# Four slots for gathered expert rows and a new timetable for scatters and expert tiles in a cross-attention and MoE kernel

## What is computed

```python
def reference(x, ctx_4096, L0_ffn_base_w, L0_ffn_base_b, L0_ffn_A, L0_ffn_B, L0_ffn_router_w):
    # x (8, 224, 2048), ctx (8, 750, 2048), base_w (2048, 2048), A (64, 2048), B (16, 2048, 64), all fp32
    def _L0_xattn_ref(query, key):
        a = jnp.einsum('bqd,bkd->bqk', query, key)
        e = jax.nn.softmax(a, axis=-1)
        return jnp.einsum('bqk,bkd->bqd', e, key)
    def _L0_ffn_ref(x, base_w, base_b, A, B, router_w):
        base_out = jnp.einsum('bsi,oi->bso', x, base_w) + base_b
        res_hidden = jnp.einsum('bsi,ri->bsr', x, A)
        probs = jax.nn.softmax(jnp.einsum('bsi,ei->bse', x, router_w), axis=-1)
        topw, topi = jax.lax.top_k(probs, 2)
        topw = topw / (jnp.sum(topw, axis=-1, keepdims=True) + 1e-06)
        combine = jnp.sum(jax.nn.one_hot(topi, 16, dtype=x.dtype) * topw[..., None], axis=-2)
        delta = jnp.einsum('bse,bsr,eor->bso', combine, res_hidden, B)
        return base_out + delta * 0.5
    x = x + _L0_xattn_ref(_layernorm(x, axis=-1), ctx_4096)
    x = x + _L0_ffn_ref(_layernorm(x, axis=-1), L0_ffn_base_w, L0_ffn_base_b, L0_ffn_A, L0_ffn_B, L0_ffn_router_w)
    return x
```

## Time and profile before

| | us |
|---|---|
| median of three runs | 1538.42 (1529.47 to 1540.98) |
| the profiled execution | 1535.22 |
| its span, first to last instruction | 1533.5 |
| PE busy | 1386.5 |
| VectorE busy | 948.0 |
| ACT busy | 630.4 |
| POOL busy | 319.4 |
| mean granted clock of TensorE | 0.957 |

### The profile page before, as it was taken

How to read it: one execution, slowest core, us unless ns; L and a number is a source line. 1 busy time by engine, 2 the same in 40 slices (tenths; PEclk the granted TensorE clock), 3 DMA queues, 4 the chain that set the end, 5 groups by cost and what they waited for, 6 DMA issues and landing times.

```text
span 1533.5 us, 18405 instructions
## 1 busy us (share of the span) xinstructions
PE 1386.5 (90%) x6777; PEld 1121.6 (73%) x6777; DVE 948.0 (62%) x1199; ACT 630.4 (41%) x797; POOL 319.4 (21%) x247
## 2 busy tenths in 40 slices
PE   5889999999999999998997779877788999999998
PEld 4668787777878787876886657755566778888886
DVE  5467777677776867774572646554557664555543
ACT  3354554545455555453210546554556621011100
POOL 1001102020202020103217323334344111111110
PEclk9989999999999999998999889888898999999999
DMA  6967778686878686695645698797886788888884
GB/s 226 272 195 248 218 245 259 206 257 209 251 236 263 218 266 215 209 218 171 196 137 159 191 300 228 201 297 209 246 260 169 250 290 262 240 240 244 259 256 130
DMA packets 216840, 350.59 MB, mean 229 GB/s; under 512 B 26992, under 2 KB 129392, under 8 KB 207088
## 3 DMA queue, kind: packets, MB, share of 16 engines
q1 hardware_dynamic: 198192, 282.31, 61.0%
q0 software_dynamic: 10528, 52.85, 11.4%
q10 hardware_dynamic: 8064, 14.68, 2.8%
HBM read 266.11 MB, written 99.41 MB: 238 GB/s over the span
## 4 chain that ended last, share of the span: by engine, by line
PE 32%; DMA 12%; DVE 4%; ACT 3%; issue 2%; POOL 2%; SPq 1%; ACTq 0%; POOLq 0%; DVEq 0%
PE scores L821 10%; PE scores L822 9%; PE scores L823 9%; DMA b_in<-in_bT_dram,brow_i 6%; DMA res<-x_scratch 4%; ACT b_hl L1029 2%; POOL hs_scratch L1566 1%; PE work L857 1%; DMA w_in<-in_wT_dram 1%; PE work L858 1%; DVE b_hl L1410 1%; DVE a_l L1368 1%; SPq L561 1%; DVE w_l L1361 1%; DMA a_in<-xT_scratch 1%
## 5 line engine op out<-in xcount | busy, mean ns | idle before, releaser
L821 PE MATMUL scores<-w_h,a_h 128*128 128x512 f32 x896 | 359.0, 401 | 60.8 <-DVE a_l L1368 56.6
L822 PE MATMUL scores<-w_l,a_h 128*128 128x512 f32 x896 | 355.1, 396 | 0.0
L823 PE MATMUL scores<-w_h,a_l 128*128 128x512 f32 x896 | 354.8, 396 | 0.0
L821 PEld LDWEIGHTS scores<-w_h,a_h 128*128 128x128 f32 x896 | 171.8, 192 | 103.8 <-DVE a_l L1368 51.3
L1014 ACT ACTIVATE a_h<-a_in 128x512 fp32r<-128x512 f32 x168 | 93.9, 620 | 314.6 <-DMA a_in<-xT_scratch 204.6
L1368 DVE TENSOR_TENSOR a_l<-a_in,a_h 128x512 fp32r<-128x512 f32 x168 | 130.4, 824 | 124.8 <-ACT a_h L1014 120.6
L823 PEld LDWEIGHTS scores<-w_h,a_l 128*128 128x128 f32 x896 | 171.2, 191 | 38.9
L822 PEld LDWEIGHTS scores<-w_l,a_h 128*128 128x128 f32 x896 | 171.8, 192 | 37.6
L691 PE MATMUL scores<-ctxT_h,nT_h 128*112 128x494 f32 (+1 forms) x512 | 175.0, 342 | 10.1 <-DVE ctxT_l L1119 6.7
L1129 DVE TENSOR_TENSOR raw_l<-raw_in,val_h 128x512 fp32r<-128x512 f32 x192 | 154.9, 826 | 45.5 <-ACT val_h L945 45.3
L790 PE MATMUL scores<-val_h,eT_h 128*112 128x512 f32 (+1 forms) x384 | 159.5, 415 | 19.2 <-DVE raw_l L1129 17.5
(11 more groups left out here) (153 smaller groups left out, 1903.6 us busy)
## 6 DMA issues: line engine op xcount, KB each, us to landing
ctxT_in<-in_ctxT_dram SPq DMA_DIRECT2D x64, 750.0 KB, 6.6
a_in<-xT_scratch SPq DMA_DIRECT2D x42, 1024.0 KB, 9.4
raw_in<-in_ctx_dram SPq DMA_DIRECT2D x32, 1280.0 KB
w_in<-in_wT_dram SPq DMA_DIRECT2D x32, 512.0 KB, 11.1
x<-in_x_dram SPq DMA_DIRECT2D x8, 1792.0 KB, 10.6
xT_scratch<-xT_st SPq DMA_DIRECT2D x8, 1792.0 KB, 11.8
res<-x_scratch SPq DMA_DIRECT2D x56, 256.0 KB, 7.9
y_add<-y_scratch SPq DMA_DIRECT2D x56, 256.0 KB, 5.5
```

The source lines that it names most:

```text
L821: pe.matmul(o, ah, wh, start=(k == 0), stop=False)
L822: pe.matmul(o, ah, wl, start=False, stop=False)
L823: last = pe.matmul(o, al, wh, start=False, stop=(k == KD - 1))
```

## The change

`b_in` spans all 128 partitions and has four slots: tiles with s % 4 of 0 and 1 use partitions 0 to 63, tiles with 2 and 3 partitions 64 to 127, and `b_hl` takes the high part on the same half and the low part on the other (`halves`). Four gathers are issued at once in the beginning, two in visit 11, and later each gather stands six tiles ahead. The 28 scatters of hidden rows stand in visits 6 to 9 instead of 7 to 10, each in the same groups of seven. The first group of hidden rows is loaded and transposed in visit 11 instead of 10, and `expert_high` and `expert_low` of tiles 0 and 1 stand ahead of `slots_high(0)` and `slots_low(0)`. Visit 11 joins `ROUTING`. The tiles of visits 11 to 15 were 3, 3, 0, 0, 4 and are 0, 2, 2, 3, 3; visits 16 to 26 keep three each.

```diff
@@ -89,6 +89,7 @@
     ACCS = 3
     SL = (2 * T + E * (P - 1)) // P
     SG = 4
+    BR = 4
     GROUPS = -(-SL // SG)
     RW = R + 1
     NOWHERE = 4096
@@ -261,7 +262,7 @@
         b_hl = over(at_x2, "b_hl", [P, 2, D], F32R)
         masked = over([at_nT[0]], "masked", [P, E, E])
         ends_at = over([at_nT[0] + 4 * E * E], "ends_at", [R, SL, E])
-        b_in = over(at_nT, "b_in", [R, 2, D])
+        b_in = over(at_nT, "b_in", [P, 2, D])
         routes = list(at_nT)
         y_out = over(at_nT, "y_out", [P, 3, D])
         s_hh = over(at_nT, "s_hh", [P, 2, SG * P], F32R)
@@ -314,6 +315,11 @@
 
         acc = [scores[:, 1, 0:BANK], scores[:, 1, BANK:2 * BANK], scores[:, 0, 0:BANK]]
         s_bank = scores[:, 0, BANK:2 * BANK]
+
+        def halves(s):
+
+            same, other = slice(0, R), slice(R, P)
+            return (same, other) if s % BR < 2 else (other, same)
 
         def y_bank(c):
             return work[:, c // 2, (c % 2) * BANK:(c % 2 + 1) * BANK]
@@ -385,7 +391,7 @@
         s_high = sem("s_high")
         s_ready = sem("s_ready")
         yrow_ready = sem("yrow_ready")
-        b_loaded = [sem(f"b_loaded{i}") for i in range(2)]
+        b_loaded = [sem(f"b_loaded{i}") for i in range(BR)]
         b_high = sem("b_high")
         b_ready = sem("b_ready")
         y_done = sem("y_done")
@@ -410,17 +416,17 @@
 
         X2T_TAIL_AT = (2, 5, 8, 11)
         HID_TAIL_AT, HN_TAIL_AT = 1, 6
-        HR_AT, ROUTE_AT, COUNT_AT, PLACE_AT, SCATTER_AT = 3, 4, 6, 6, (7, 8, 9, 10)
-        Y_FIRST_AT = 10
-        ROUTING = (ROUTE_AT, ROUTE_AT + 1, PLACE_AT)
+        HR_AT, ROUTE_AT, COUNT_AT, PLACE_AT, SCATTER_AT = 3, 4, 6, 6, (6, 7, 8, 9)
+        Y_FIRST_AT = 11
+        ROUTING = (ROUTE_AT, ROUTE_AT + 1, PLACE_AT, Y_FIRST_AT)
 
         Y_TILES, n = {}, 0
-        for g in (11, 12) + tuple(range(TT + 1, 2 * TT - 1)):
-            count = min(4 if g == TT + 1 else 3, SL - n)
+        for g in range(TT - 2, 2 * TT - 1):
+            count = min(2 if g < TT else 3, SL - n)
             Y_TILES[g] = list(range(n, n + count))
             n += count
         assert n == SL
-        Y_BEHIND = {3: (3, 8, 13), 4: (2, 6, 10, 14)}
+        Y_BEHIND = {2: (4, 11), 3: (3, 8, 13)}
 
         LATE_TILES, n = {}, 0
         for g in range(2 * TT, GT):
@@ -1024,9 +1030,10 @@
                 act.activation(s_hh[R:P, n % 2, cols], s_bank[0:R, cols], ACT.Copy).then_inc(s_high, 1)
 
             def expert_high(s):
-                act.wait_ge(b_loaded[s % 2], (s // 2 + 1) * 16)
+                act.wait_ge(b_loaded[s % BR], (s // BR + 1) * 16)
                 at_least(act, y_done, (s - 1) * NC)
-                act.activation(b_hl[0:R, s % 2, :], b_in[:, s % 2, :], ACT.Copy).then_inc(b_high, 1)
+                same, other = halves(s)
+                act.activation(b_hl[same, s % 2, :], b_in[same, s % 2, :], ACT.Copy).then_inc(b_high, 1)
 
             def rows_out(s):
 
@@ -1089,9 +1096,9 @@
                     act.wait_ge(route, 2)
                     act.activation(t16[1][:, :, :], t16[0][:, :, :], ACT.Exp).then_inc(rexp_done, 1)
                 if g == Y_FIRST_AT:
-                    slots_high(0)
                     expert_high(0)
                     expert_high(1)
+                    slots_high(0)
                 for s in Y_TILES.get(g, []):
                     if s % SG == 2 and s // SG + 1 < GROUPS:
                         slots_high(s // SG + 1)
@@ -1407,7 +1414,8 @@
 
             def expert_low(s):
                 dve.wait_ge(b_high, s + 1)
-                dve.tensor_tensor(b_hl[R:P, s % 2, :], b_in[:, s % 2, :], as_f32(b_hl[0:R, s % 2, :]),
+                same, other = halves(s)
+                dve.tensor_tensor(b_hl[other, s % 2, :], b_in[same, s % 2, :], as_f32(b_hl[same, s % 2, :]),
                                   ALU.subtract).then_inc(b_ready, 1)
 
             def rows_out(s):
@@ -1483,9 +1491,9 @@
                 if g == PLACE_AT:
                     run_place()
                 if g == Y_FIRST_AT:
-                    slots_low(0)
                     expert_low(0)
                     expert_low(1)
+                    slots_low(0)
                 for s in Y_TILES.get(g, []):
                     if s % SG == 2 and s // SG + 1 < GROUPS:
                         slots_low(s // SG + 1)
@@ -1567,13 +1575,14 @@
                                         hg[:, i, t, :], None).then_inc(hs_scattered, 16)
 
             def load_expert(s):
-                if s >= 2:
-                    pool.wait_ge(b_ready, s - 1)
+                if s >= BR:
+                    pool.wait_ge(b_ready, s - BR + 1)
                 else:
                     pool.wait_ge(route, PLACED)
-                pool.indirect_dma_start(b_in[:, s % 2, :], None, bT.rearrange("e r d -> (e r) d"),
+                same, other = halves(s)
+                pool.indirect_dma_start(b_in[same, s % 2, :], None, bT.rearrange("e r d -> (e r) d"),
                                         bass.IndirectOffsetOnAxis(ap=brow_i[:, s:s + 1], axis=0)
-                                        ).then_inc(b_loaded[s % 2], 16)
+                                        ).then_inc(b_loaded[s % BR], 16)
 
             def scatter_out(s):
                 pool.wait_ge(y_left, (s + 1) * (NC - 1))
@@ -1622,19 +1631,19 @@
                     if g == SCATTER_AT[0]:
                         pool.wait_ge(route, PLACED)
                         pool.wait_ge(fresh_stored, 16)
-                        load_expert(0)
-                        load_expert(1)
+                        for s in range(BR):
+                            load_expert(s)
                     per = -(-2 * TT // len(SCATTER_AT))
                     first = SCATTER_AT.index(g) * per
                     for n in range(first, min(first + per, 2 * TT)):
                         scatter_rows(n // TT, n % TT)
                 if g == Y_FIRST_AT:
-                    load_expert(2)
-                    load_expert(3)
+                    load_expert(BR)
+                    load_expert(BR + 1)
                 for s in Y_TILES.get(g, []):
                     scatter_out(s)
-                    if s + 4 < SL:
-                        load_expert(s + 4)
+                    if s + BR + 2 < SL:
+                        load_expert(s + BR + 2)
 
 
 _INS = ["x", "ctx_4096", "L0_ffn_base_b"]
```

## The result

The changed kernel takes 1473.93 us, the median of four runs (1472.64 to 1478.73); the kernel before, on the same chip, 1534.84 (1529.47 to 1540.98). The ratio is 0.9608, 95% interval 0.956 to 0.9656: 61 us less, where 78 were forecast. The profiled execution took 1478.73 us with a span of 1477.0, which is 56.5 us under the span before.

The account below looks back on a forecast made before the run. PE, busy 90% of the span, bounds the kernel; losses are its waits and the low clock behind them. Visits 16 to 26 give -56 and visits 10 to 15 -22, sum -78 us: 1459, range 1430 to 1499.

Parts of the forecast that it names:

- Four slots, the wait for `a_l`: Visits 16 to 26: gathers issued four tiles ahead remove nearly all of PE's `a_l` wait; -56 us for the stretch.
- The third rival: POOL, held by `res`, still issues gathers late; visits 16 to 26 stay at 23.6 us, total 1516; chance 0.06.
- The other half of the partitions: `b_hl` copies on ACT and VectorE: using the other 64 partitions costs nothing, staying at 1.92 and 2.30 us.
- What is late next: Visits 16 to 26: next wait is for a `y_out` slot, freed by a scatter behind `add_bias` and `res`; 18.5 us per visit.
- the formula: Visit length T = R + L - 5.1 where over 16.7 us; R is the time of `res`, L of the scatter.
- T = 18.5: Forecast length in us of each of visits 16 to 26, 203.5 in all; ends 16.7 and 22.
- Scatters one visit sooner: Visits 10 and 11: hidden rows scattered earlier and first used later, removing PE's 15.4 us `hs` wait and some 4 at low clock.
- Tiles spread: Visits 11 to 15: expert tiles beside chunk 1's weight pairs and loads cost 15 us, top 30; visits 10 to 15 net -22.
- PE alone: First rival: `y_out` slots come free in time and PE's own work sets the visits; -105 us, 1433; chance 0.18.
- Crowded DMA: Second rival: DMA share reaches 0.95, `res` and scatters near 13.5 us each, weight loads slow too; 1490 to 1510; chance 0.14.
- slower loop of `y_out`: Fourth rival: longest `res` and scatter times make visits 29.6 us, +44 in all, 1581; decides from R + L = 30.7; chance 0.04.

Follow-up runs that it names:

- slots alone: The changed kernel with the old timetable put back, so only four slots and the longer gather lead remain: 1495.07 us, 0.974 of the kernel before.
- timetable alone: The changed kernel with two `b_in` slots instead of four, keeping the new timetable: 1519.14 us, 0.990 of the kernel before.
- the kernel with half of the scattered bytes and the new order: Changed kernel without scatters of second-choice rows, with `add_bias` last on POOL and the `hs` load ahead of `res` on SyncE: 1441.26 us.

## Why the prediction was nearly right

Its stretches against the profile of after, in us:

| | forecast | measured | off by |
|---|---|---|---|
| up to visit 10 | 824.1 | 826.2 | +2.1 |
| visits 10 to 13 and 15 | 73.7 | 68.6 | -5.1 |
| visit 14 | 26.3 | 39.0 | +12.7 |
| visits 16 to 26 | 203.5 | 215.8 | +12.3 |
| from visit 27 | 327.5 | 327.3 | -0.2 |

(26.3 is the counted 16.3 and the 4, 5 and 1 us of the prediction for visit 14; 73.7 is the rest of its 100.) That is 22 us more in the profiled execution, the slowest of the four. The medians are 15 apart, 1459 forecast and 1474 measured, and all four runs lie in the range. The 2 us up to visit 10 say nothing, as that start lies anywhere in 7 us in the other profiles.

*Four slots, the wait for `a_l`.* Right in mechanism and place. The wait is gone with four slots (slots alone: -47 us in visits 16 to 26) and there in full with two (timetable alone: 48.3 us). The third rival, that the lead is eaten up by late gathers, is out: gathers take 10.7 us in the middle now, not 8.0, and PE waits for none.

*The other half of the partitions.* Right: all 43 `b_hl` of ACT take 1.90 to 1.92 us on either half. VectorE's take 2.29 in the middle, as before; a few of up to 3.85 make their average 2.39, which no wait of PE shows.

*What is late next.* Right: it is the slot of `y_out` behind the scatter behind `add_bias` behind `res`, and the formula holds where it binds. From the start of visit 19, 0.6 + 18.9 + 2.7 + 4.8 + 0.6 is 27.6, less the 7.9 that PE can go, which makes 19.7 for a visit that else took 16.5: a wait of 3.2, and PE's was 2.9. (POOL's 2.7 us are 1.6 in the forecast.) **The step that failed is its size, T = 18.5.** It has 1.8 us of waiting in each of eleven visits, 20 in all, and the profile has 215.9 - 195.7 = 20.2 us of idle time. That this agrees is in part luck: R is 19 to 22 or about 7 and not in between, the four long waits behind a late `res` make 14.8 us, and the other 5.4 are short waits that the formula does not have. Missing is what a wait does to the clock. PE's 195.7 us of work are 185.7 for the same instructions in the kernel with half of the scattered bytes and the new order, at a granted clock of 1.00. So **10.0 us at low clock** are most of the error of the term, and 2.4 more are a count that was too short (792 matmuls at 0.227 and eight transposes at 0.44 are 183.3). I had counted the clock where I removed waits, and not where I left some.

*Scatters one visit sooner.* Right to a us or two: the last one is issued at 839.79 (forecast 838), PE's transposes start at 847.28, and PE waits for nothing there. The runs with the old timetable, 15.4 and 22.1 us of that wait, show that it is the timetable that removes it.

*Tiles spread.* Right that this part costs something at visit 14, and its first wait is the one that was worked out: PE waits 4.2 us for a `w_l` that VectorE ends at 882.4, 19.1 us after visit 13 began (forecast 4 and 18.9). (The prediction counts the group of transposes of this visit in visit 15, which shifts 0.4 us between the two and leaves their sum.) The bank of `y_out` behind the pairs is 3.3 us instead of 5. **What failed is the load of the weights.** I had three us for it, in visit 15; it takes 18.6 to 28.0 us and stands in visit 14: 7.3 us more of waiting, and 7.4 of low clock where I had one. The top of my own range for this step (30 instead of 15) had this very case; visits 10 to 15 took 23 us more than their count of 85, between the two. Where no gather and no scatter are issued beside the loads, they take 9.5 to 12.7 us and the visit 18.8. Where tiles are taken out of visits 13 and 14 but the last ones of visit 12 are still issued beside the loads, they take 15.7 to 21.2 us and the visit 24.6. With half of the scattered bytes it is 32.9 and 32.1. So the transfers beside the loads make these late, and late loads are a good part of the long visit; how much is gathers, scatters, `a_in` or SyncE's queue is open, and so is what else keeps the visit at 32 us when the loads come sooner.

*The rivals.* PE alone (1433) needs what, in visits 16 to 26, only the kernel with half the scattered bytes and the new order has. (The "second case below" in the prediction's lines on the Trainium skill can only mean this rival, which it lists first.) Crowded DMA (1490 to 1510) is right in part of the cause and too dear: the DMA share is 0.94 in visits 16 to 26, where I had 0.95 as its mark, but this costs 12 us more than forecast there and 13 in visit 14, not 31 to 51 in all. In the slower loop of `y_out` R + L stayed at 27.2 or less in visits 16 to 26.

*My theory of what is left*, that POOL's order alone holds the scatters up, fell: changing the order brought some 4 us where 15 and more were expected, no more than the runs' spread. PE's full speed in visits 16 to 26 came only where order and bytes both changed. Why one kernel's runs spread over 26 us with that order (1458.85 to 1484.62) stays open, and the cause given above for the slow `res` of every second visit is read from the times and not tested.

What the prediction named as signs: no wait for `a_l`, no gather in the chain, no wait for `hs`, ACT waiting for `y_scratch` (41.0 us), PE for `w_l` at visit 14, all there. Not there: visits of 17 to 20 us without pairs (16.5 to 24.4, alternating), and a clock above 0.95 (0.93 over the 17 visits, 0.95 in the last eleven). Of the signs of a wrong step one came, visits in pairs still, though by the loop of `y_out` and no longer by the gathers.

## What to carry to other kernels

When a wait is replaced by a shorter one, price the clock behind the shorter one too; here 20 us of waiting left 10 us of low clock behind it. When transfers are given more lead or moved, look at what else lands in the stretch into which they move, above all loads that are issued as late as they can be. And where an edit to an order removes a wait but not the time, halve the bytes in both orders: the two runs show how much of what is left is order and how much is bytes.

## What the runs showed of the hardware

Packets of gathers and scatters (8 KB) take 309 ns at the tenth percentile and 638 at the ninetieth in visits 16 to 26, and 309 and 641 in the same visits before. These two times are the same at a DMA share of 0.94 and of 0.78, so most of the difference is not the crowd's. That packets get longer where queues meet shows elsewhere in the changed kernel's trace: the 512-byte packets of SyncE's queue take 31 ns on average while no 8 KB packet is under way, and 51 while four to seven are; the 8 KB packets themselves go from 406 to 438 ns on average with as many of the small ones. So the same share of busy time can stand for more or fewer bytes, and a share near one is no sign of a stall by itself: it is 0.97 at 244 GB/s in the kernel with half of the scattered bytes and the new order, where PE stands still for 0.8 us in these visits, and 0.98 at 281 GB/s in one where it stands still for 11.4. The Trainium skill ("DMA: Bandwidth & Descriptors", Queues, rings and completion order) says that each DMA engine goes round the queues that have work, packet by packet. By this rule a load must slow down when gathers are put beside it, and the weights do: 9.5 to 12.7 us without and 18.6 to 28.0 with. The turns of single engines no trace here shows.

The same page (Rules for kernel authors) holds that two transfers to separate halves of the partitions share the same engines, so that nothing is won by it. The trace agrees in that the gathers, now on both halves, are no quicker: their middle time rose from 8.0 to 10.7 us, at a DMA share that rose from 0.78 to 0.94 in visits 16 to 26. ACT's and VectorE's copies cost the same on either half. No run has four slots on one half; that the gain is that of the slots rests on the wait that went, which was for late gathers.

SyncE is not free while it issues. In visit 14 the issue of one `res` took 23.91 us, and the load of `hs` stood behind it:

```profile
863.87 1.83 SPq L567 DMA_DIRECT2D res<-x_scratch  x1
...
866.22 11.06 SPq L544 DMA_DIRECT2D w_in<-in_wT_dram  x7
878.34 0.55 SPq L557 DMA_DIRECT2D a_in<-xT_scratch  x1
878.93 23.91 SPq L567 DMA_DIRECT2D res<-x_scratch  x1
902.88 0.44 SPq L609 DMA_DIRECT2D hs<-hs_scratch  x1
```

The same issue takes 1.83 us at 863.87, when the queues are nearly empty (a DMA share of 0.05 in the 2.5 us before it). The time of such an issue is a part of R that no list of waits shows. The run with `res` first shows that the order on SyncE doesn't do away with it: there the load behind `a_in` is held, whichever it is.
